# Keys and values first, activations and leaf sums in PSUM, and another order of the last down products

## The chip, the cores and the metric

One Trainium2 chip; the kernel runs on one core. The metric is the device time of one execution in microseconds (us). TensorE is PE, VectorE DVE, ScalarE ACT, GpSimd POOL, SyncE (which here only starts transfers) SP.

## The reference, cut to what matters

```python
def unit_projection(x):                     # query, keys, values
    f = jnp.fft.fft(x); f = f / (jnp.abs(f) + 1e-08); return jnp.fft.ifft(f).real
query = unit_projection(x @ Wq.T + bq)      # x: layernormed, 2 x 4096 x 512
keys, values = unit_projection(x @ Wk.T + bk), unit_projection(x @ Wv.T + bv)
s = jnp.cumsum(bind(keys, values), axis=1)  # bind: product of the spectra
x1 = x0 + unbind(s, query)                  # times the conjugate spectrum
logits = layernorm(x1) @ W_in.T + b_in      # 8 trees of 255 nodes, depth 7
# in each tree, walk from the root by (logit > 0); keep silu(logit) on the path
out = x1 + (silu(logits) * on_path) @ W_out.T
```

## The kernel before, in words

The kernel works through 8192 tokens in NB = 32 blocks of T = 256 (J = 2 halves of 128). Each engine has a program of its own, written out by hand and coupled to the others by semaphores only: `first()` is the prologue, `step(0)`, a loop of steps 1 to 29, and `step(30)`, `step(31)`. In step i a block's feed-forward part runs beside the spectral part of block n = i+1. Nothing reorders an engine's instructions, so the order of the calls is the schedule.

**PE** in a step: `project` for the three groups Q, K, V (144 matmuls into two banks `bank_p`, emptied by ACT's `evac_re` and `evac_im`); `logits(i, t, c)` for tree t, half c (12 matmuls each into `bank_l[t % 4]`), between them `counts(i, t)`, which puts nodes off the path out of play according to the decisions `dec`; `nyquist_rows` and `nyquist_sums` (a few tiny matmuls for one frequency that is handled apart); `down(i, j)`, 42 matmuls for each half j into `bank_l[j]`; then `inverse_transform` into `bank_i[j]`. Operands are split into a high and a low float16 part, and products of three pairs summed: thus the pairs of names `a_hi`/`a_lo`, `xn_pair`, `z_hi`/`z_lo`.

**DVE** in a step: `residual` (x1 = input + inverse transform), statistics and normalisation to `xn2` (L1107), `low` (L1126, the low part of the split), `decide` (L1219, `dec` from the logits), `act_low` (L1226, the low part of the activations), the spectral `q_inverse`, `kv_denominator`, `kv_inverse`, `k_scale` (L1136 to L1154), `running_sum` (L1199, L1202), `next_stats` (layernorm of block n+1), `leaf_dots` (L1239) and `leaf_add` (L1249) for two of the eight trees, whose 128 leaves are not multiplied densely: the row of the reached leaf is fetched by an indirect transfer of POOL into `fetched`, its logit is a dot product with `xn2`, and its output row is added to x1. `result` (L1287) adds the down product, and SP stores it.

**ACT** in a step: the copies out of `bank_p`, squares (L749) and roots (L753), the high halves of splits (L721), `leaf` (L761), `silu(i, t)` (L794) from `bank_l` into `acts`, a ring of HELD = 3 in SBUF, and `act_high` (L804) from `acts`. Sqrt and Silu lie in different function tables: a load of a table (ACT_TABLE_LOAD) stands before the first silu and before the first Sqrt of a step. **POOL** sums squares, forms `bind`, `q_unit`, `unbind`, and starts the fetches.

**Waits that matter.** Normalised halves reach PE through SP's transposing transfers, `xt` (spectral) and `x2t` (feed-forward): `logits(i, 0, 0)` waits for `x2t`, whose transposes wait for `low`; `project(n+1, .)` waits for `xt`. `logits` of tree t reuses `bank_l[t % 4]`, so trees 4 to 7 wait for `silu` of tree t-4 (`act_ready`), `counts(i, t)` for `decide(i, t)`, `down` for `act_low`.

**The prologue** transforms the weights by the DFT on PE (`bias_fold`, `fold_tile`; L473 and L478 spread the largest weight over the partitions), scales and splits W_in and W_out into high and low parts (ACT `win_high`, `wout_high`, L811; DVE `win_low`, `wout_low`, L1327; four pieces each), and does the spectral part of block 0 (`first_bind`, `first_unbind`, `first_z_low` at L1399).

## Time and profile before

| | |
|---|---|
| time before, median of 3 runs | 1904.76 us (1904.72 to 1905.31) |
| the profiled execution's own time | 1902.03 us |
| its span in the profile | 1899.9 us |
| PE busy | 1846.0 us, 97% of the span |
| DVE, ACT, POOL busy | 1548.9, 1117.4, 943.0 us |
| mean granted clock of PE | 0.989 of full speed |

The span runs from the first to the last recorded instruction; the profiled execution's own time has 2.1 us around it. A line is busy time, not importance: PE sets the time wherever it is not idle, and for the rest one has to see what it waits for.

### The profile page before, as it was taken

How to read it: one execution, taken by the hardware profiler on the slowest of the kernel's cores; microseconds unless marked ns; L12 is line 12 of the kernel's file. 1: busy time of each engine (PE TensorE's matmuls, PEld its weight loads, DVE VectorE, ACT ScalarE, POOL GpSimd, SP SyncE). 2: the span in 40 equal slices, each digit the busy share in tenths (PEclk: the TensorE clock that was granted, in tenths of full speed). 3: DMA queues.
4: the chain of work that ended last, by engine and by line, in shares of the span. 5: the costliest groups of instructions: out<-in, count | busy, mean ns of one | idle time of the engine just before them, and what ended most of it. 6: DMA issues, size and time to landing. Idle time of an engine off the chain costs nothing.

```text
span 1899.9 us, 40007 instructions
## 1 busy us (share of the span) xinstructions
PE 1846.0 (97%) x14488; PEld 1389.5 (73%) x14488; DVE 1548.9 (82%) x2938; ACT 1117.4 (59%) x2151; POOL 943.0 (50%) x737
## 2 busy tenths in 40 slices
PE   8499999999999999999999999999999999999978
PEld 6478777778777778877777877777877777787755
DVE  4888888888888888888888888888888888888783
ACT  5666565566565556656556656556655555665643
POOL 1254445564445565444556445556544556545450
PEclk9799999999999999999999999999999999999999
DMA  8032232222133222223222213322223322222312
GB/s 288 12 87 79 68 100 92 74 88 88 55 100 100 70 85 88 73 82 100 79 87 87 85 59 100 98 68 88 88 59 96 100 77 77 88 69 86 89 56 67
DMA packets 181785, 163.18 MB, mean 86 GB/s; under 512 B 140161, under 2 KB 140801, under 8 KB 181761
## 3 DMA queue, kind: packets, MB, share of 16 engines
q1 hardware_dynamic: 163328, 95.48, 17.0%
q0 software_dynamic: 18432, 67.38, 10.7%
q8 instruction: 15, 0.25, 0.1%
q14 instruction: 10, 0.07, 0.0%
HBM read 95.72 MB, written 16.78 MB: 59 GB/s over the span
## 4 chain that ended last, share of the span: by engine, by line
PE 90%; DVE 2%; DMA 1%; ACT 1%; issue 0%; SPq 0%; DVEq 0%; ACTq 0%
PE bank_l L532 31%; PE bank_l L589 30%; PE bank_p L482 23%; PE bank_l L542 3%; PE bank_i L482 2%; DMA arena<-xn_pair 1%; PE bank_i L553 1%; PE bank_i L560 0%; SPq L341 0%; DVE xn_pair L1126 0%; DVE arena L1239 0%; ACT xn_pair L721 0%; ACT arena L794 0%; PE bank_i L559 0%; DVE arena L1249 0%
## 5 line engine op out<-in xcount | busy, mean ns | idle before, releaser
L532 PE MATMUL bank_l<-arena,win_mem 128*128 128x256 f16 x5376 | 625.1, 273 | 16.5 <-DMA arena<-xn_pair 16.5
L589 PE MATMUL bank_l<-wout_mem,arena 128*128 128x512 f16 x2688 | 593.4, 379 | 0.0
L532 PEld LDWEIGHTS bank_l<-arena,win_mem 128*128 128x128 f16 x5376 | 525.0, 98 | 80.5 <-DMA arena<-xn_pair 15.1
L482 PE MATMUL bank_p<-arena,wf_hi 128*128 128x256 f16 x3072 | 505.8, 273 | 2.7 <-ACT arena L740 2.7
L589 PEld LDWEIGHTS bank_l<-wout_mem,arena 128*128 128x128 f16 x2688 | 260.6, 98 | 308.8 <-DVE arena L1226 11.7
L482 PE MATMUL bank_p<-arena,wf_lo 128*128 128x256 f16 x1536 | 419.0, 273 | 0.0
L985 POOL TENSOR_TENSOR arena<-arena 128x512 f32<-128x512 f32 x96 | 121.8, 1269 | 553.1 <-ACT arena L749 553.1
L482 PEld LDWEIGHTS bank_p<-arena,wf_hi 128*128 128x128 f16 x3072 | 299.6, 98 | 37.6 <-ACT arena L740 3.0
L1226 DVE SCALAR_TENSOR_TENSOR arena<-arena,s_act 128x512 f16<-128x512 f32 (+1 forms) x256 | 238.7, 942 | 80.4 <-ACT arena L804 66.3
L794 ACT ACTIVATE arena<-bank_l,bias_in,s_logit 128x256 f32<-128x256 f32 x448 | 229.2, 554 | 121.4 <-PE bank_l L542 121.0
L1219 DVE TENSOR_SCALAR dec<-bank_l,thr,off 128x256 bf16<-128x256 f32 x256 | 136.0, 542 | 92.5 <-PE bank_l L532 91.0
L1066 POOL DMA_INDIRECT arena<-in_leaf_rows,leaf_row x128 | 140.3, 1096 | 109.4 <-issue 70.5
L804 ACT ACTIVATE arena<-arena,s_act 128x512 f16<-128x512 f32 (+1 forms) x256 | 166.6, 664 | 3.2
L482 PEld LDWEIGHTS bank_p<-arena,wf_lo 128*128 128x128 f16 x1536 | 150.5, 98 | 17.5
L1136 DVE RECIPROCAL arena<-arena 128x256 f32<-128x256 f32 x64 | 111.9, 1748 | 61.8 <-POOL arena L990 61.8
L1126 DVE TENSOR_TENSOR xn_pair<-arena,xn_pair 128x512 f16<-128x512 f32 x128 | 143.3, 1142 | 9.5 <-ACT xn_pair L721 9.5
L1239 DVE SCALAR_TENSOR_TENSOR arena<-arena 128x512 f32<-128x512 f32 x128 | 142.7, 1167 | 0.9 <-DMA arena<-in_leaf_rows,leaf_row 0.9
L990 POOL TENSOR_SCALAR arena<-arena,eps_s 128x512 f32<-128x512 f32 x64 | 45.4, 709 | 133.3 <-ACT arena L753 130.3
L1148 DVE RECIPROCAL arena<-arena 128x256 f32<-128x256 f32 x64 | 107.7, 1725 | 1.1
L714 ACT ACTIVATE arena<-arena 128x512 f16<-128x512 f32 x31 | 19.5, 630 | 149.1 <-POOL arena L1030 149.1
L726 ACT ACTIVATE arena<-bank_p,bias_f 128x256 f32<-128x256 f32 x192 | 80.5, 470 | 42.0 <-PE bank_p L482 42.0
L749 ACT ACTIVATE arena<-arena 128x1024 f32<-128x1024 f32 x96 | 101.5, 1057 | 5.3
(175 smaller groups left out, 2500.6 us busy)
## 6 DMA issues: line engine op xcount, KB each, us to landing
arena<-in_x SPq DMA_DIRECT2D x32, 512.0 KB, 3.5
arena<-arena SPq DMA_DIRECT2D x32, 512.0 KB, 2.9
out<-arena SPq DMA_DIRECT2D x64, 256.0 KB, 2.1
wout_mem<-in_w_in_t SPq DMA_DIRECT2D x1, 3584.0 KB, 16.1
arena<-in_w_out_t SPq DMA_DIRECT2D x1, 3584.0 KB, 13.8
arena<-xn_pair SPq DMA_TRANSPOSE x128, 2.8
arena<-in_leaf_rows,leaf_row POOLq DMA_INDIRECT x128, 5.7
win_mem<-in_wq SPq DMA_DIRECT2D x1, 1024.0 KB, 7.5
```

The source lines that it names most:

```text
L482: mm = pe.matmul(bank, a, b, start=(n == 0), stop=(n == len(pairs) - 1))
L532: mm = pe.matmul(bank_l[t % 4][:, c * T:(c + 1) * T], a[:, k, w:w + P], x2t[:, :, b, k, :], start=(c == 0 and k == 0 and m == 0), stop=((t ...
L589: mm = pe.matmul(bank_l[j][:, :], a[:, m, tok], w[:, m, :], start=(m == 0 and a is a_hi and w is wout_hi), stop=(m == DENSE - 1 and a is a ...
L794: ins = act.activation(acts[:, t % HELD, c * T:(c + 1) * T], bank_l[t % 4][:, c * T:(c + 1) * T], ACT.Silu, bias=bias_in[:, c, t:t + 1], s ...
L804: act.activation(a_hi[:, m:m + wide, :], acts[:, t % HELD, 0:wide * T].rearrange("p (c t) -> p c t", c=wide), ACT.Copy, scale=s_act[:, 0:1 ...
L985: pool.tensor_tensor(mag[:, q].rearrange("p c t -> p (c t)"), sq[:, 0:2].rearrange("p c t -> p (c t)"), sq[:, 2:4].rearrange("p c t -> p ( ...
L1066: pool.indirect_dma_start(fetched[:, g, j, :], None, leaf_rows, bass.IndirectOffsetOnAxis(leaf_row[:, g, j:j + 1], 0)).then_inc(leaf_fetch ...
L1126: dve.tensor_tensor(xn_pair[:, j, 1, :], xn[:, j, :], xn_pair[:, j, 0, :], ALU.subtract).then_inc(done, 1)
L1136: dve.reciprocal(mag[:, Q, h], mag[:, Q, h]).then_inc(rinv_ready, 1)
L1219: dve.tensor_scalar(dec[:, t % HELD, :], bank_l[t % 4][:, 0:T], thr[:, t:t + 1], off[:, 0:1], ALU.is_gt, ALU.mult).then_inc(dec_ready, 1)
L1226: dve.scalar_tensor_tensor(out=a_lo[:, m, :], in0=acts[:, t % HELD, 0:wide * T].rearrange("p (c t) -> p c t", c=wide), scalar=s_act[:, 0:1 ...
L1239: ins = dve.scalar_tensor_tensor(out=row, in0=row, scalar=1.0, in1=xn2[:, j, :], op0=ALU.mult, op1=ALU.mult, accum_out=leaf_dot[:, g, j:j ...
```

## The change

- **Group order.** K, V, Q in place of Q, K, V: in the prologue's loads, in `project`, in the spectral work. In the prologue the unbinding is done with the raw query spectrum (`first_unbind`, POOL `first_sums`), and the query's inverse size multiplied in afterwards (`first_unit`).
- **Activations in PSUM.** `acts` is gone: `silu` writes back into `bank_l[t % 4]`, `act_high` and `act_low` read it there; trees 4 to 7 therefore wait for `act_low` of tree t-4 (`a_lo_ready`).
- **xn2 and the leaf sums in PSUM.** `xn2` lies in `bank_i`. `leaf_add` sums into `total` in `bank_l[2 + j]`, begun by an ACT copy of x1 (`begin_total`). `leaf_add(i)` and `result(i)` move into DVE's next step: one `leaf_add` ahead of `residual`, the rest behind `low2`.
- **Down.** Each half is cut in two: trees 0 to 5 of half 0, `counts` 6 and 7, trees 0 to 5 of half 1, then trees 6 and 7 of both. Counts and logits interleave in another order.
- **ACT.** `std(n + 1)` (a Sqrt) moves from ahead of the first silu to between `act_high(4)` and `silu(5)`.
- **Prologue.** All W_out splitting moves out of the prologue into block 0; two W_in pieces of DVE move behind `first_z_low`.
- **SP.** In step i the transposes of `xt` for n+1 now come first and those of `x2t` for block n follow, so that the latter no longer stand behind another copy and load.

The diff, cut to its core (12 leading spaces taken off):

```diff
-HELD = 3
+HELD = 4
...
-Q, K, V, G_IN, G_OUT = range(5)
+K, V, Q, G_IN, G_OUT = range(5)
...
-        sp_size = bank_i[1][:, 16:16 + 3 * J].rearrange("p (j q) -> p j q", q=3)
+        xn2 = [bank_i[j][:, :] for j in range(J)]
+        total = [bank_l[2 + j][:, :] for j in range(J)]
+        sp_rows = bank_p[1][:, 0:3 * J].rearrange("p (j q) -> p j q", q=3)
...
+sp.dma_start(wnat_s[:, K], wk.rearrange("(k p) d -> p k d", p=P)).then_inc(proj_in[K], 16)
 sp.dma_start(dft_s, dft.rearrange("(k p) f -> p k f", p=P)).then_inc(dft_in, 16)
-sp.dma_start(b_nat[:, :, :], b_qkv).then_inc(dft_in, 16)
+sp.dma_start(b_nat[:, :, :], b_kvq).then_inc(dft_in, 16)
+sp.dma_start(xa, x_v[0]).then_inc(x_loaded, 16)
+sp.dma_start(wnat_s[:, V], wv.rearrange("(k p) d -> p k d", p=P)).then_inc(proj_in[V], 16)
 sp.dma_start(wnat_s[:, Q], wq.rearrange("(k p) d -> p k d", p=P)).then_inc(proj_in[Q], 16)
-sp.dma_start(xa, x_v[0]).then_inc(x_loaded, 16)
-sp.dma_start(wnat_s[:, K], wk.rearrange("(k p) d -> p k d", p=P)).then_inc(proj_in[K], 16)
-sp.dma_start(wnat_s[:, V], wv.rearrange("(k p) d -> p k d", p=P)).then_inc(proj_in[V], 16)
...
-    project(0, Q)
+    project(0, K)
...
+    project(0, V)
     for m in range(1, KT):
-        fold_tile(V, m)
-    project(0, K)
-    project(0, V)
+        fold_tile(Q, m)
+    project(0, Q)
...
-    peak_to_all(G_OUT)
     pe.wait_ge(z_hi_ready, 2)
     pe.wait_ge(z_lo_ready, 2)
+    for j in range(J):
+        inverse_transform(j)
+    peaks_in_row(G_OUT)
     pe.wait_ge(sp_carry_ready, 1)
-    for j in range(J):
-        inverse_transform(j)
...
     if attn:
+        project(n, K)
+    if isinstance(i, int) and i == 0:
+        peak_to_all(G_OUT)
+    if attn:
+        project(n, V)
+    if attn:
         project(n, Q)
-        project(n, K)
-        project(n, V)
     logits(i, 0, 0)
+    logits(i, 2, 0)
+    counts(i, 0)
     logits(i, 1, 0)
-    counts(i, 0)
-    logits(i, 2, 0)
     logits(i, 2, 1)
     logits(i, 3, 0)
+    if attn:
+        nyquist_rows(n)
     logits(i, 3, 1)
     counts(i, 1)
+    counts(i, 2)
     logits(i, 4, 0)
+    logits(i, 4, 1)
+    counts(i, 3)
+    logits(i, 5, 0)
+    logits(i, 5, 1)
     leaf_rows_of(i, 0)
-    if attn:
-        nyquist_rows(n)
-    logits(i, 4, 1)
-    logits(i, 5, 0)
-    counts(i, 2)
-    logits(i, 5, 1)
-    counts(i, 3)
+    counts(i, 4)
     logits(i, 6, 0)
+    counts(i, 5)
     logits(i, 6, 1)
-    if attn:
-        nyquist_sums(n)
-    counts(i, 4)
-    counts(i, 5)
     logits(i, 7, 0)
     logits(i, 7, 1)
+    down(i, 0, range(0, 6))
     counts(i, 6)
-    down(i, 0)
-    down(i, 1)
+    counts(i, TREES - 1)
+    if attn:
+        nyquist_sums(n)
+    down(i, 1, range(0, 6))
+    down(i, 0, range(6, TREES))
+    down(i, 1, range(6, TREES))
     if attn:
         transform_back(i)
...
+def high2(n, j):
+    act.wait_ge(ln2_done, J * n + j + 1)
+    act.activation(xn_pair[:, j, 0, :], xn2[j], ACT.Copy).then_inc(xn2_hi_ready, 1)
+def begin_total(i, j):
+    act.wait_ge(a_lo_ready, TREES * i + 7 + j)
+    act.activation(total[j], x1[:, j, :], ACT.Copy).then_inc(total_begun, 1)
...
-    if t >= HELD:
-        act.wait_ge(a_lo_ready, TREES * i + t + 1 - HELD)
-    elif not isinstance(i, int) or i:
-        act.wait_ge(a_lo_ready, TREES * i)
     for c in [c for c in range(2) if (t, c) in COLUMN]:
-        ins = act.activation(acts[:, t % HELD, c * T:(c + 1) * T], bank_l[t % 4][:, c * T:(c + 1) * T],
+        ins = act.activation(bank_l[t % 4][:, c * T:(c + 1) * T], bank_l[t % 4][:, c * T:(c + 1) * T],
...
     act.activation(a_hi[:, m:m + wide, :],
-                   acts[:, t % HELD, 0:wide * T].rearrange("p (c t) -> p c t", c=wide), ACT.Copy,
+                   bank_l[t % 4][:, 0:wide * T].rearrange("p (c t) -> p c t", c=wide), ACT.Copy,
...
-    for c in range(PIECES):
+    for c in range(3):
         wout_rows(c)
-    high(1, xn1, ln1_done, xn1_hi_ready)
     act.wait_ge(z_sum, 1)
     act.activation(z_hi[:, 0:2, :], prod[:, 0], ACT.Copy).then_inc(z_hi_ready, 1)
     act.activation(z_hi[:, 2:4, :], prod[:, 2], ACT.Copy).then_inc(z_hi_ready, 1)
-    wout_high(0)
-    wout_high(1)
+    wout_rows(3)
...
+    if isinstance(i, int) and i == 0:
+        wout_high(0)
+    if attn:
+        square(n, K)
+        evac_im(n, V)
+        square(n, V)
         evac_re(n, Q)
+        root(n, K)
+    if isinstance(i, int) and i == 0:
+        wout_high(1)
+    if attn:
...
+        act.wait_ge(ffn_consts_done, 1)
     if isinstance(i, int) and i == 0:
         wout_high(2)
         wout_high(3)
...
+    silu(i, 0)
     if isinstance(i, int) and i == 0:
-        act.wait_ge(ffn_consts_done, 1)
-    leaf(i, 0)
-    if nxt:
-        std(n + 1, mv1, rs1, ln1_mv, ln1_std)
-    if attn:
-        root(n, V)
-    if isinstance(i, int) and i == 0:
-        act.wait_ge(wout_lo_done, PIECES)
-    silu(i, 0)
+        act.wait_ge(wout_hi_done, 1)
+        act.wait_ge(wout_lo_done, 1)
+    act_high(i, 0)
+    if attn:
+        nyquist_size(n)
+    silu(i, 1)
     leaf(i, 1)
-    act_high(i, 0)
-    silu(i, 1)
-    if attn:
-        nyquist_size(n)
+    act_high(i, 1)
     silu(i, 2)
-    act_high(i, 1)
     act_high(i, 2)
     silu(i, 3)
     leaf_row_copy(i, 0)
+    silu(i, 4)
     act_high(i, 3)
-    silu(i, 4)
     act_high(i, 4)
     if nxt:
+        std(n + 1, mv1, rs1, ln1_mv, ln1_std)
+    silu(i, 5)
+    if nxt:
         shifted(n + 1)
-    silu(i, 5)
     act_high(i, 5)
     silu(i, 6)
     act_high(i, 6)
-    silu(i, 7)
     if nxt:
         act.wait_ge(x2t_ready, 16 * J * (i + 1))
         high(n + 1, xn1, ln1_done, xn1_hi_ready)
+    silu(i, 7)
     act_high(i, 7)
+    begin_total(i, 0)
     if attn:
         z_high(n)
     leaf_silu(i, 0)
+    begin_total(i, 1)
     leaf_silu(i, 1)
 steps(act, first, step)
...
+        sum_squares(n, Q)
+        add_eps(n, Q)
+        bind(n)
         q_unit(n)
-        bind(n)
-    fetch(i, 1)
-    fetch(i, 0)
+    for g in range(LEAVES):
+        fetch(i, g)
...
-                             in0=acts[:, t % HELD, 0:wide * T].rearrange("p (c t) -> p c t", c=wide),
+                             in0=bank_l[t % 4][:, 0:wide * T].rearrange("p (c t) -> p c t", c=wide),
...
-    nyquist_den(0)
-    kv_denominator(0)
-    nyquist_inverse(0)
-    kv_inverse(0, 0)
-    nyquist_unit(0)
     kv_inverse(0, 1)
...
-    low(1, xn1, xn1_hi_ready, xn1_lo_ready)
...
     running_sum(0)
-    peak_row(G_OUT)
     first_unbind()
+    q_inverse(0, 0)
+    q_inverse(0, 1)
+    first_unit()
+    nyquist_den(0)
+    nyquist_inverse(0)
+    nyquist_unit(0)
+    nyquist_bind(0)
+    first_z_low()
+    win_low(2)
...
-    feed_forward_constants()
-    first_z_low()
-    wout_low(0)
-    wout_low(1)
...
+    begun = not isinstance(i, int) or i > 0
+    if begun:
+        leaf_add(i - 1, 0)
+    residual_of(i, 0)
+    if isinstance(i, int) and i == 0:
+        peak_row(G_OUT)
+    residual_of(i, 1)
+    stats2(i)
+    if isinstance(i, int) and i == 0:
+        win_low(3)
+        scale_group(G_OUT)
+    normalise2(i)
+    low2(i)
+    if isinstance(i, int) and i == 0:
+        feed_forward_constants()
+        wout_low(0)
+        wout_low(1)
+    if begun:
+        leaf_add(i - 1, 1)
+        result(i - 1, 0)
+        result(i - 1, 1)
+    if attn:
+        kv_denominator(n)
+    if isinstance(i, int) and i == 0:
+        dve.wait_ge(ffn_consts_done, 1)
+    decide(i, 0)
+    if attn:
+        kv_inverse(n, 0)
+        kv_inverse(n, 1)
+    decide(i, 1)
     if isinstance(i, int) and i == 0:
         wout_low(2)
+    decide(i, 2)
+    if attn:
+        q_inverse(n, 0)
+    if isinstance(i, int) and i == 0:
+        dve.wait_ge(wout_lo_done, 2)
+    act_low(i, 0)
+    if isinstance(i, int) and i == 0:
         wout_low(3)
     if attn:
-        q_inverse(n, 0)
+        k_scale(n)
+        nyquist_den(n)
+    act_low(i, 1)
+    decide(i, 3)
+    if attn:
+        q_inverse(n, 1)
+        nyquist_inverse(n)
+    decide(i, 4)
+    act_low(i, 2)
+    decide(i, 5)
+    if attn:
+        nyquist_unit(n)
     if nxt:
         next_stats(n + 1)
-    decide(i, 0)
-    decide(i, 1)
-    if attn:
-        q_inverse(n, 1)
-        kv_denominator(n)
-        kv_inverse(n, 0)
-        kv_inverse(n, 1)
-        k_scale(n)
-    act_low(i, 0)
-    decide(i, 2)
-    decide(i, 3)
-    if attn:
-        nyquist_den(n)
-        nyquist_inverse(n)
-        nyquist_unit(n)
-    decide(i, 4)
-    decide(i, 5)
+    act_low(i, 3)
+    act_low(i, 4)
+    decide(i, 6)
+    if attn:
+        nyquist_bind(n)
     if nxt:
         scale_and_shift(n + 1)
-    act_low(i, 1)
-    if attn:
-        nyquist_bind(n)
-    act_low(i, 2)
-    act_low(i, 3)
-    decide(i, 6)
     if attn:
         running_sum(n)
-    act_low(i, 4)
+    act_low(i, 5)
     decide(i, 7)
-    act_low(i, 5)
     act_low(i, 6)
     if attn:
         nyquist_unbind(n)
+    leaf_dots(i, 0)
     act_low(i, 7)
+    if attn:
+        nyquist_carry(n)
     if nxt:
         low_of(n + 1, 0, xn1, xn1_hi_ready, xn1_lo_ready)
-    if attn:
-        nyquist_carry(n)
-    if nxt:
         low_of(n + 1, 1, xn1, xn1_hi_ready, xn1_lo_ready)
-    leaf_dots(i, 0)
     leaf_dots(i, 1)
-    leaf_add(i, 0)
     if attn:
         carries(n)
-    leaf_add(i, 1)
-    result(i, 0)
-    result(i, 1)
-steps(dve, first, step)
+def last():
+    for g in range(LEAVES):
+        leaf_add(NB - 1, g)
+    result(NB - 1, 0)
+    result(NB - 1, 1)
```

What stands on the engines now, at three places. **DVE in block 0**, from `low` of the feed-forward layernorm to the first `decide` (L1219, after: L1293); `wout_mem<-arena,sc,wout_mem` is `wout_low`. Before:

```order
L1126 TENSOR_TENSOR xn_pair<-arena,xn_pair 128x512 [waits xn2_hi_ready] x2
L1327 SCALAR_TENSOR_TENSOR wout_mem<-arena,sc,wout_mem 128x1792 [waits scaled,wout_hi_done] x2
L1136 RECIPROCAL arena<-arena 128x256 [waits den_ready]
L1094 BN_STATS st1<-arena 128x6 [waits x_loaded]
L1094 BN_STATS st1<-arena 128x6
L1100 BN_AGGR mv1<-st1 128x2 [waits ln1_stat]
L1100 BN_AGGR mv1<-st1 128x2
L1219 TENSOR_SCALAR dec<-bank_l0,thr,off 128x256 [waits logit_full]
L1219 TENSOR_SCALAR dec<-bank_l1,thr,off 128x256 [waits logit_full]
```

After:

```order
L1404 SCALAR_TENSOR_TENSOR wout_mem<-arena,sc,wout_mem 128x1792 [waits scaled,wout_hi_done] x2
L1216 SCALAR_TENSOR_TENSOR arena<-arena,eps_s 128x512 [waits root_ready,den_ready]
L1293 TENSOR_SCALAR dec<-bank_l0,thr,off 128x256 [waits logit_full,ffn_consts_done]
L1222 RECIPROCAL arena<-arena 128x256 [waits kv_den_ready] x2
L1293 TENSOR_SCALAR dec<-bank_l1,thr,off 128x256 [waits logit_full]
L1404 SCALAR_TENSOR_TENSOR wout_mem<-arena,sc,wout_mem 128x1792 [waits scaled,wout_hi_done]
L1293 TENSOR_SCALAR dec<-bank_l2,thr,off 128x256 [waits logit_full]
L1210 RECIPROCAL arena<-arena 128x256 [waits den_ready]
L1300 SCALAR_TENSOR_TENSOR arena<-bank_l0,s_act,arena 128x256 [waits a_hi_ready,wout_lo_done]
```

Two `wout_low` stand ahead of the first `decide` still, but nothing of them is done in the prologue any more; the feed-forward constants came to this place too.

**ACT in step 0** (the loop's body reads the same there), around the Sqrt on `mv1` that belongs to the next layernorm. Before:

```order
L761 ACTIVATE on_leaf<-bank_l0,one,off_inv 128x256 [waits leaf_row_full,count_full]
L693 ISA
L694 ACTIVATE rs1<-mv1,ln_eps 128x2 [waits ln1_mv]
L753 ACTIVATE arena<-arena 128x512 [waits ss_ready]
L794 ACT_TABLE_LOAD [waits a_lo_ready]
L794 ACTIVATE arena<-bank_l0,bias_in,s_logit 128x256 [waits count_full]
```

After, between `act_high(4)` and `silu(5)`:

```order
L838 ACTIVATE arena<-bank_l3,s_act 128x512 [waits act_ready]
L838 ACTIVATE arena<-bank_l0,s_act 128x512 [waits act_ready]
L712 ISA
L713 ACT_TABLE_LOAD
L713 ACTIVATE rs1<-mv1,ln_eps 128x2 [waits ln1_mv]
L826 REGISTER_ALU
L828 ACT_TABLE_LOAD
L828 ACTIVATE bank_l1<-bank_l1,bias_in,s_logit 128x256 [waits count_full]
```

The Sqrt stood among other Sqrts; now it stands between silus, with a table load on either side of it.

**PE at the end of step 0**: the down matmuls are L589 (after: L597), the counts L542 (after: L554). Before:

```order
L589 MATMUL bank_l0<-wout_mem,arena 128x512 [waits a_lo_ready]
L589 MATMUL bank_l0<-wout_mem,arena 128x512 x5
L542 MATMUL bank_l3<-dec,path 128x256 [waits dec_ready]
L542 MATMUL bank_l3<-dec,path 128x256
L589 MATMUL bank_l0<-wout_mem,arena 128x512 [waits a_lo_ready]
L589 MATMUL bank_l0<-wout_mem,arena 128x512 x5
L589 MATMUL bank_l0<-wout_mem,arena 128x512 [waits a_lo_ready]
L589 MATMUL bank_l0<-wout_mem,arena 128x512 x5
```

After:

```order
L597 MATMUL bank_l0<-wout_mem,arena 128x512 [waits a_lo_ready]
L597 MATMUL bank_l0<-wout_mem,arena 128x512 x5
L554 MATMUL bank_l2<-dec,path 128x256 [waits dec_ready]
L554 MATMUL bank_l2<-dec,path 128x256
L554 MATMUL bank_l3<-dec,path 128x256 [waits dec_ready]
L554 MATMUL bank_l3<-dec,path 128x256
L568 MATMUL bank_p1<-sp_kv,running 128x3 [waits sp_kv_ready]
L569 MATMUL bank_p1<-sp_kv,running 128x3
L597 MATMUL bank_l1<-wout_mem,arena 128x512 [waits a_lo_ready,wout_lo_done,wout_hi_done]
L597 MATMUL bank_l1<-wout_mem,arena 128x512 x29
L597 MATMUL bank_l0<-wout_mem,arena 128x512 [waits a_lo_ready]
L597 MATMUL bank_l0<-wout_mem,arena 128x512 x5
L597 MATMUL bank_l0<-wout_mem,arena 128x512 [waits a_lo_ready]
```

Trees 6 and 7 of half 0 (the rows with waits at the end) now come behind 30 matmuls of half 1.

## Rows read from the trace of the kernel before

**Rows 1.** PE's waits: waited for, us in total, times, longest us.

```profile
PE bank_l L532 <- DMA arena<-xn_pair: 16.5, 5, 14.1
PE bank_l L473 <- DVE mxp L1297: 11.7, 1, 11.7
PE bank_i L482 <- DVE arena L1399: 6.4, 1, 6.4
PE bank_p L434 <- DVE b_pair L1406: 5.1, 1, 5.1
PE bank_i L553 <- ACT arena L740: 4.6, 1, 4.6
PE bank_p L482 <- ACT arena L740: 2.7, 1, 2.7
```

**Rows 2.** Windows; us, busy (x) of PE PEld DVE ACT POOL, clock, DMA share, GB/s.

```profile
60.20:90.00 29.80, 5.84 (x39) 5.06 (x38) 26.93 (x53) 19.32 (x25) 2.97 (x3) 0.57 0.08 18
90.00:109.41 19.41, 16.72 (x147) 14.44 (x145) 16.08 (x35) 12.76 (x22) 2.55 (x3) 0.96 0.34 83
109.41:149.98 40.57, 40.57 (x307) 28.52 (x305) 36.43 (x58) 22.80 (x45) 27.81 (x21) 1.00 0.21 66
302.37:1822.00 1519.63, 1517.52 (x12080) 1143.95 (x12078) 1266.07 (x2395) 906.21 (x1776) 798.35 (x619) 1.00 0.27 83
```

**Rows 3.** The chain that ended last, two steady blocks: start us, us, work.

```profile
358.68 15.65 PE bank_l L589 x72
375.69 15.72 PE bank_p L482 x144
415.00 15.65 PE bank_l L589 x72
```

**Rows 4.** Timeline of DVE in the prologue.

```profile
9.31 1.23 DVE L1293 TENSOR_TENSOR arena<-win_mem 128x1024 f32<-128x1024 f32 x1 [4.34 <-DMA win_mem<-in_wq]
```

**Rows 5.** DVE by line and form: busy us, mean ns | idle before.

```profile
L1226 DVE SCALAR_TENSOR_TENSOR arena<-arena,s_act 128x512 f16<-128x512 f32 x192 | 207.9, 1096 | 74.2 <-ACT arena L804 60.2 <-issue 13.9
L1219 DVE TENSOR_SCALAR dec<-bank_l,thr,off 128x256 bf16<-128x256 f32 x256 | 136.0, 542 | 92.5 <-PE bank_l L532 91.0
L1136 DVE RECIPROCAL arena<-arena 128x256 f32<-128x256 f32 x64 | 111.9, 1748 | 61.8 <-POOL arena L990 61.8
L1327 DVE SCALAR_TENSOR_TENSOR win_mem<-wout_mem,sc,win_mem 128x1792 f16<-128x1792 f32 x4 | 9.9, 2486 | 1.9 <-ACT win_mem L811 1.9
L1327 DVE SCALAR_TENSOR_TENSOR wout_mem<-arena,sc,wout_mem 128x1792 f16<-128x1792 f32 x4 | 8.2, 2083 | 0.9 <-ACT wout_mem L811 0.9
```

**Rows 6.** ACT by line and form: busy us, mean ns | idle before.

```profile
L794 ACT ACT_TABLE_LOAD x32 | 41.1, 1283 | 0.6
L721 ACT ACTIVATE xn_pair<-arena 128x512 f16<-128x512 f32 x128 | 73.3, 621 | 27.9 <-DVE arena L1107 27.9
L811 ACT ACTIVATE wout_mem<-arena,sc 128x1792 f16<-128x1792 f32 x4 | 6.9, 1777 | 0.2 <-DVE sc L1320 0.2
```

**Rows 7.** Timeline of DVE in a steady block: start us, us, work.

```profile
248.00 0.21 DVE L1184 SCALAR_TENSOR_TENSOR sp_z<-bank_i,sp_carry,sp_hat 128x2 f32<-128x2 f32 x1
249.31 1.79 DVE L1226 SCALAR_TENSOR_TENSOR arena<-arena,s_act 128x512 f16<-128x512 f32 x1 [1.10 <-ACT arena L804]
...
278.50 1.22 DVE L1094 BATCH_NORM_STATS2 st<-arena 128x6 f32<-128x512 f32 x2
...
280.13 0.54 DVE L1219 TENSOR_SCALAR dec<-bank_l,thr,off 128x256 bf16<-128x256 f32 x1
...
411.96 0.73 DVE L1226 SCALAR_TENSOR_TENSOR arena<-arena,s_act 128x512 f16<-128x512 f32 x1
```

**Rows 8.** Timeline of POOL at the same time as the first two of rows 7.

```profile
247.61 1.60 POOL L1022 TENSOR_TENSOR arena<-arena 128x512 f32<-128x512 f32 x1
```

**Rows 9.** Timeline of ACT around a table load.

```profile
282.73 0.63 ACT L753 ACTIVATE arena<-arena 128x512 f32<-128x512 f32 x1 [0.22 <-POOL arena L985]
283.38 1.28 ACT L794 ACT_TABLE_LOAD   x1
```

336 lines of the change are left out of this document (187 added, 149 removed).

## The prediction

> **What bounds the kernel now.** I looked first at the table of time and busy shares: PE is busy for 1846.0 of 1899.9 us, so at most 53.9 us can be won while its matmuls stay as they are, and the change takes no matmul away. Next, PE's waits [rows 1]. The reader is to see that nearly all of them happen once: seven or eight single waits of the prologue, 11.7 us for the largest weight of W_out (L473) at their head, and one of 14.1 us, which is the last block, where no projection of a next block hides its normalisation. Of the 16.5 us on `x2t` only 16.5 - 14.1 = 2.4 are spread over four steady blocks. Then the windows [rows 2]: from 302.37 to 1822.00 PE is idle for 1519.63 - 1517.52 = 2.1 us. From 60.20 to 90.00 it is busy for 5.84 of 29.80 us, and its granted clock is 0.57 there, near its lower level of 1.2 GHz; DVE is busy for 26.93 of them. So DVE bounds that stretch, and PE the rest. The chain [rows 3] gives the steady period: 415.00 - 358.68 = 56.32 us.
>
> So the steady blocks have almost nothing to give, and thirty of them multiply whatever goes wrong: 0.1 us a block is 3 us. The prologue can give some.
>
> **Part 1, the prologue.** The order of waits is the DVE's. Before, PE starts the folds once DVE has done the query rows, the first at 9.31 [rows 4], behind a wait for the transfer of wq; after, wk is loaded first and the DFT table second, the bias fold needs the latter, and I let it start at the same point as before plus 0.4 us (it waits longest of the loads now). Before, PE had finished the folds and all of `project(0)` at 60.20 [rows 2]. After, the same matmuls run in another order, with the query group last, and it waits for the last `fold_low` of the query weights, which by DVE's order I place at 57.4, a stall of about 2.3 us: the end is 60.2 + 0.4 + 2.3 = 62.9.
>
> DVE from 57.4, by the durations of its own rows [rows 5] and of those like them: `kv_inverse` 1.75, `k_scale` 1.2, `first_bind` 2.4, the scans 2.7, `first_unbind` 2.5, two `q_inverse` of 1.75 and a short wait 3.7, `first_unit` 1.2, the Nyquist terms 0.9, z 2.7 with ACT's part between: 19.05, of which I take 18.4, since PE, POOL and ACT overlap a little at the joints. The transform begins at 75.8 and takes 1.4 with some reloads; `project(1, K)` starts at about 79.2, where `project(1, Q)` stood at 90.0 [rows 2]: a gain of **10.8 us**. A cross-check from what leaves DVE's stretch: four `win_low` of 2.49 us, of which two come earlier, beside PE's work, and two later; a normalisation and its split, 2.4; the peak of W_out, about 1.5; and two reciprocals of the query come in, 3.5: -9.9 - 2.4 - 1.5 + 3.5 = -10.3. With it go PE's wait of 11.7 us for W_out's peak and the 1.2 and 6.4 after it [rows 1]; one wait of PE for z takes their place.
>
> **Part 2, block 0 pays for it.** What left the prologue is not gone: four `wout_low` of 2.08 us, four `wout_high` of 1.78 us and two `win_low` lie in block 0 [rows 5, 6]. Where do they stand on PE's path?
> - ACT has `wout_high(0)` and one square ahead of `evac_im` of V and `evac_re` of Q: PE waits about 2.35 us for its bank, where it waited 2.7 before [rows 1]. Even.
> - DVE has `wout_low(0)` and `(1)` and the constants ahead of `decide(0)`: 4.2 us, of which 2 lie beside two sets of logits. Stall at `counts(0)` 2.25 us. What is queued behind: `decide(1)` and (2).
> - `decide(2)` stands behind `wout_low(2)`: 0.2 us. `act_low(0)`, which `logits(4)` now waits for since the activations lie in the bank itself, stands behind `wout_high(2)`, `(3)` on ACT and behind the reciprocal of Q on DVE: 1.9 us.
> - `decide(3)` stands behind `wout_low(3)`, `k_scale` and `act_low(1)`: 1.7 us.
>
> That sums to 6.05 us; before, the same block had no wait at all from 109.41 to 149.98 (PE busy 40.57 of 40.57) [rows 2]. Net of prologue and block 0: -10.8 - 0.35 + 6.05 = -5.1, and I take **-4.8** (POOL's tensor work is at its heaviest in that block). Bounds: if all six are hidden -11; if each wait comes out half as long again, and the fold starts 2 us late, 0.
>
> **Part 3, the steady block: what is removed.** Trees' activations, xn2 and the leaf sums come from PSUM. DVE's `act_low` takes 1.096 us in the mean but 0.73 when it is alone [rows 5, 7]. The trace shows who stretches it: at 249.31 an `act_low` with two SBUF inputs took 1.79 us beside POOL's tensor operations, but at 248.00, inside POOL's 1.60 us operation, one with an input in PSUM took 0.21 [rows 7, 8], as its mean elsewhere. So with `acts` in PSUM `act_low` should take 0.73 to 0.8 throughout: 6 of 1.1 become 6 of 0.75, 2 us of DVE a block; `low2` and `leaf_dots` gain likewise, another 1 to 1.5. The rate on a large tile is not shown by a 2-column row; its bounds are 0.73 and 1.1.
>
> The Trainium skill ("SBUF — State Buffer", section "Who interferes with whom") says that a DVE instruction with two SBUF inputs contends with a GpSimd instruction that reads SBUF, and one with at most one SBUF input does not; by that rule the lower bound holds, and the trace's 0.21 us agrees.
>
> All this is off the path, since PE is the bound. What PE gets of it is only the 2.4 us of `x2t` waits: `low2` ends about 0.8 us earlier (`result` and half of the `leaf_add` no longer stand ahead of `residual`; `leaf_add(0)` alone does), and the transposes no longer stand behind the copy and the load on SP's queue. **-2.4**.
>
> **Part 4, the steady block: what is added.** Two more table loads of 1.28 us [rows 6, 9] and two copies of x1 at 0.6 (like the 0.62 of L721) on ACT: 3.8 us a block, on an engine that is busy for 59%. And several tighter waits. From the start of project at t = 0: 144 matmuls 15.72 us [rows 3], so 0.109 each; 12 matmuls of a logits half 1.31, counts 0.22. Then `logits(7, 0)` is due at 15.7 + 12 x 1.31 + 6 x 0.22 + 0.5 = 33.3. It waits for `act_low(3)`; before, it waited for `silu(3)` only, an operation and a half earlier. DVE's chain to it: `logits(5, 1)` ends at 30.2, `decide(5)` 0.2 + 0.5, Nyquist 0.1, `next_stats` 1.63 (280.13 - 278.50) [rows 7], `act_low(3)` 0.73: 33.3. There is no slack. `counts(3)` has 0.1 to 0.2, `logits(4)` and `(6)` 0.5 each. These are sums of ten terms, so their error is some 0.2 us, and a stall of 0.1 repeats 30 times. I take 0.03 a block, **+1**; bounds 0 and 0.4 a block (12 us).
>
> ACT's load before `silu(5)` delays `act_high(5)` and `act_low(5)`, for which tree 5 of `down` on half 0 waits. By the same count it is due 1.4 us after it is ready: that is the cover, and each us beyond it costs 30.
>
> The Trainium skill ("ScalarE: Activation LUTs", section "What ACT_TABLE_LOAD costs") prices a switch at about 1.28 us plus 1.38 us of drain, 2.66 together, and so speaks against two more switches a block. The trace shows the load alone: the root ends at 283.36, the load runs from 283.38 for 1.28 us [rows 9]. By the page, ACT would have 2.8 us more in each block and `act_low(5)` would be late by 1.2 us.
>
> **Part 5, the tail.** The last block's 14.1 us stay; its normalisation writes PSUM and one `leaf_add` precedes its residual: **+0.3**, bounds 0 and 0.6.
>
> **Sum.** -4.8 - 2.4 + 1 + 0.3 = -5.9 against the profiled execution's 1902.03, and the median of the runs shown is 2.7 us above that. 1904.76 - 5.9 = 1898.9; I say **1899.2** (-0.3%). A difference of 0.2%, 3.8 us, is about what a measurement of this kernel can tell from none.
>
> **Rivals.**
> - *A, the orders hold* (forecast): 1895 to 1902. For it: the period is PE's and the slacks add up to zero or more. Chance 0.5.
> - *B, block 0 pays less.* Its waits are mostly hidden since the starts of ACT and DVE move forward with the earlier PE: 4 to 7 us less, 1892 to 1895. Against: the DVE work there is a sum of known durations. Chance 0.1.
> - *C, small loss.* The chain to `logits(7, 0)` or `counts(3)` is 0.1 to 0.2 us late per block (3 to 6 us), or the prologue gains half: 1902 to 1908. For it: slack 0.0. Chance 0.18.
> - *D, the DVE queue becomes the bound* between `decide(5)` and `act_low(3)` (slower side). Place: `next_stats` ahead of `act_low(3)`. It decides from 0.2 us late a block on; at 0.4 it costs 12: 1911. What speaks for it: four banks are now held until `act_low`, where a ring of three and the bank were before. Against: `act_low` from PSUM is alone in 0.73. Chance 0.14.
> - *E, ACT's extra work shows.* If a table switch took the longer of the two times above, or PSUM operands gave no relief from POOL (`leaf_dots(1)` and the split for `xt` then end 1 to 1.5 us late for the transform), 30 blocks lose 1 to 1.5 us each: 1930 to 1945. Against: 283.38 and 248.00. Chance 0.08.
>
> **How the numbers follow.** Faster by over 0.2% (under 1901.0): most of A and all of B, 0.55. Within 0.2%: the rest of A and the first half of C, 0.20. Slower (over 1908.6): the end of C, D and E, 0.25. The range reaches from B's end, 1892, to D's, 1911, and leaves out E and the far part of D.
>
> **What the profile after would show.** Right: the wait of 11.7 us is gone and the first transform begins near 76, after one wait for z; PE waits in block 0 for `dec` and `a_lo`, 6 us in all; `act_low` 128x512 at 0.73 to 0.8 in the mean; PE's period 56.32 still, no repeated wait over 0.1 us; 4 table loads a block of 1.28, each following at once. Wrong: a wait of PE on `act_low` or `decide` 30 times, above all at `logits(7, 0)`; a wait for `z_lo` or `xt` at the end of each block; `act_low` still at 1.1.

## The result, and the profile after

The changed kernel took 1891.05 us in the median of 5 runs (1890.91 to 1896.20), the kernel before 1904.76 (1903.68 to 1905.51): ratio 0.9935, 95% interval 0.9921 to 0.995. In a second series it was 1892.61 against 1903.96, ratio 0.9945 (0.9931 to 0.9959). So the change gives 11 to 14 us, 0.6 to 0.7%, where 5.6 were forecast. The profiled execution took 1893.18 us, its span is 1891.4. The ratios are formed without two slow runs, one of the kernel before (3646.56 us, in the second series) and one of the kernel with the DFT table first (6878.83 us).

The page after, busy time and instructions; beside the table of before: PE 4 us less with the same instructions, DVE 180 us less, ACT 109 us more.

```profile
PE 1842.0 (97%) x14488; PEld 1391.5 (74%) x14488; DVE 1368.7 (72%) x2938; ACT 1226.1 (65%) x2275; POOL 866.8 (46%) x737
```

PE's waits after (us in total, times, longest), which answer to [rows 1]:

```profile
PE bank_l L544 <- DMA arena<-xn_pair: 14.6, 1, 14.6
PE bank_p L568 <- DVE sp_kv L1253: 10.2, 1, 10.2
PE bank_p L442 <- DVE b_pair L1494: 9.1, 1, 9.1
PE bank_l L554 <- DVE dec L1293: 4.1, 2, 2.8
PE bank_p L491 <- issue: 1.9, 1, 1.9
PE bank_l L544 <- DVE arena L1300: 1.7, 1, 1.7
PE bank_p L562 <- ACT arena L778: 1.6, 1, 1.6
PE bank_p L491 <- ACT arena L778: 1.0, 1, 1.0
PE bank_i L491 <- DVE arena L1482: 0.6, 1, 0.6
```

Every wait is a single one, or two in block 0. Of `x2t` (L544) only the last block's is left. The wait of 10.2 us is PE's wait in the prologue for the spectral terms of the one frequency that is handled apart, behind the whole chain of DVE; it takes the place of the one for z.

I cut both traces at the same events: the start of the first projection, of the second, of the third (block 0 lies between the last two) and of the last one. Windows of the kernel before, then after (us; busy and instructions of PE, PEld, DVE, ACT, POOL; granted clock):

```profile
34.10:89.95 55.85, 31.89 (x226) 26.13 (x224) 41.94 (x73) 35.20 (x49) 12.01 (x7) 0.77 0.18 56
89.95:149.89 59.94, 57.25 (x450) 42.91 (x449) 52.47 (x92) 35.56 (x67) 30.36 (x23) 0.99 0.25 71
149.89:1785.22 1635.33, 1633.48 (x12996) 1230.67 (x12994) 1364.30 (x2582) 977.12 (x1914) 860.63 (x667) 1.00 0.27 84
```

```profile
37.69:83.16 45.47, 31.12 (x224) 25.00 (x222) 36.83 (x62) 33.43 (x50) 8.39 (x7) 0.84 0.12 30
83.16:148.35 65.19, 58.38 (x451) 42.87 (x451) 49.17 (x101) 41.90 (x72) 28.03 (x23) 0.98 0.22 66
148.35:1775.83 1627.48, 1627.48 (x12996) 1232.65 (x12993) 1198.72 (x2581) 1081.34 (x2030) 794.41 (x667) 1.00 0.29 84
```

| stretch | before | after | difference | forecast |
|---|---|---|---|---|
| start to first projection | 34.10 | 37.69 | +3.6 | +0.4 |
| first to second projection | 55.85 | 45.47 | -10.4 | -11.2 |
| block 0 | 59.94 | 65.19 | +5.25 | +5.7 |
| 29 steady blocks | 1635.33 | 1627.48 | -7.85 | -1.4 |
| last block and end | 114.6 | 115.5 | +0.9 | +0.3 |

The sum is -8.5, the difference of the spans. The forecast column adds up to -6.2; the -5.9 of the forecast has 0.3 us more for block 0, put on by judgment. In the 29 steady blocks PE never idles after (1627.48 of 1627.48), and each lasts 56.12 us, where it was 56.32 [rows 3]. The chain after, the downs from tree 0 of half 1 on and the projections (start us, us, work; 416.08 - 359.96 = 56.12):

```profile
359.96 11.67 PE bank_l L597 x54
373.00 15.72 PE bank_p L491 x144
416.08 11.67 PE bank_l L597 x54
```

Groups of DVE and ACT by line and form, which answer to [rows 5, 6]: `act_low` takes 0.743 us in the mean (1.096 before). The loads of function tables are 62 + 31 + 30, four in a steady block, in place of 32 + 31, two in a block; each still takes 1.283 us.

```profile
L1300 DVE SCALAR_TENSOR_TENSOR arena<-bank_l,s_act,arena 128x512 f16<-128x512 f32 x192 | 139.9, 743 | 209.6 <-ACT arena L838 208.3 <-issue 1.3
```

```profile
L828 ACT ACT_TABLE_LOAD x62 | 79.5, 1283 | 1.1
L940 ACT ACT_TABLE_LOAD x31 | 39.8, 1283 | 0.6
L713 ACT ACT_TABLE_LOAD x30 | 38.5, 1283 | 0.5
```

### The profile page after: what moved, and what is told of

It is laid out like the page before. It is cut to its first block, busy times and chain, and to the rows that moved or that the text cites. A ratio compares the mean times of both kernels' runs of the same rounds, so it can differ in the third digit from the quotient of the medians.

```text
span 1891.4 us, 39940 instructions
## 1 busy us (share of the span) xinstructions
PE 1842.0 (97%) x14488; PEld 1391.5 (74%) x14488; DVE 1368.7 (72%) x2938; ACT 1226.1 (65%) x2275; POOL 866.8 (46%) x737
## 4 chain that ended last, share of the span: by engine, by line
PE 93%; DVE 3%; issue 1%; ACT 0%; DMA 0%; POOL 0%; SPq 0%; DVEq 0%; ACTq 0%
PE bank_l L597 31%; PE bank_l L544 31%; PE bank_p L491 25%; PE bank_l L554 3%; PE bank_i L491 2%; PE bank_p L562 1%; PE bank_p L569 0%; DVE arena L1210 0%; DVE wout_mem L1404 0%; DVE win_mem L1404 0%; PE bank_p L568 0%; DVE arena L1222 0%; ACT wout_mem L845 0%; DMA arena<-xn_pair 0%; DVE bank_i L1186 0%
## 5 line engine op out<-in xcount | busy, mean ns | idle before, releaser
L544 PE MATMUL bank_l<-arena,win_mem 128*128 128x256 f16 x5376 | 624.7, 273 | 16.4 <-DMA arena<-xn_pair 14.6
L597 PE MATMUL bank_l<-wout_mem,arena 128*128 128x512 f16 x2688 | 590.5, 379 | 0.0
L544 PEld LDWEIGHTS bank_l<-arena,win_mem 128*128 128x128 f16 x5376 | 526.5, 98 | 78.3 <-DMA arena<-xn_pair 15.1
L597 PEld LDWEIGHTS bank_l<-wout_mem,arena 128*128 128x128 f16 x2688 | 263.2, 99 | 302.9
L1024 POOL TENSOR_TENSOR arena<-arena 128x512 f32<-128x512 f32 x96 | 123.1, 1282 | 677.9 <-ACT arena L787 677.9
L828 ACT ACTIVATE bank_l<-bank_l,bias_in,s_logit 128x256 f32<-128x256 f32 x448 | 225.2, 536 | 187.8 <-PE bank_l L554 184.8
L1300 DVE SCALAR_TENSOR_TENSOR arena<-bank_l,s_act,arena 128x512 f16<-128x512 f32 (+1 forms) x256 | 167.8, 666 | 238.2 <-ACT arena L838 236.8
L1293 DVE TENSOR_SCALAR dec<-bank_l,thr,off 128x256 bf16<-128x256 f32 x256 | 133.2, 524 | 46.1 <-PE bank_l L544 46.1
L1114 POOL DMA_INDIRECT arena<-in_leaf_rows,leaf_row x128 | 133.0, 1039 | 72.5 <-ACT leaf_row L810 38.1
L838 ACT ACTIVATE arena<-bank_l,s_act 128x512 f16<-128x512 f32 (+1 forms) x256 | 158.4, 633 | 4.3
L1076 POOL TENSOR_TENSOR arena<-arena 128x512 f16<-128x512 f32 x62 | 93.3, 1523 | 70.5 <-ACT arena L733 70.5
L1343 DVE SCALAR_TENSOR_TENSOR fold<-bank_i,sp_z,odd 128x64 f32<-128x64 f32 (+1 forms) x128 | 35.4, 277 | 102.4 <-ACT odd L758 93.5
L758 ACT ACTIVATE odd<-bank_i 128x256 f32<-128x256 f32 x64 | 24.6, 384 | 128.8 <-PE bank_i L491 128.8
L1047 POOL TENSOR_TENSOR arena<-arena 128x512 f32<-128x512 f32 x31 | 39.3, 1267 | 128.1 <-DVE arena L1228 128.1
```

The costliest lines, as they stand in the source:

```text
L544: mm = pe.matmul(bank_l[t % 4][:, c * T:(c + 1) * T], a[:, k, w:w + P], x2t[:, :, b, k, :], start=(c == 0 and k == 0 and m == 0), stop=((t ...
L597: mm = pe.matmul(bank_l[j][:, :], a[:, m, tok], w[:, m, :], start=(m == 0 and a is a_hi and w is wout_hi), stop=(m == DENSE - 1 and a is a ...
L828: ins = act.activation(bank_l[t % 4][:, c * T:(c + 1) * T], bank_l[t % 4][:, c * T:(c + 1) * T], ACT.Silu, bias=bias_in[:, c, t:t + 1], sc ...
L838: act.activation(a_hi[:, m:m + wide, :], bank_l[t % 4][:, 0:wide * T].rearrange("p (c t) -> p c t", c=wide), ACT.Copy, scale=s_act[:, 0:1] ...
L1024: pool.tensor_tensor(mag[:, q].rearrange("p c t -> p (c t)"), sq[:, 0:2].rearrange("p c t -> p (c t)"), sq[:, 2:4].rearrange("p c t -> p ( ...
L1114: pool.indirect_dma_start(fetched[:, g, j, :], None, leaf_rows, bass.IndirectOffsetOnAxis(leaf_row[:, g, j:j + 1], 0)).then_inc(leaf_fetch ...
```

## Experiments

Two questions: where the 0.20 us a steady block come from, and why the start pays another amount than worked out. The theory after the first reading: in the kernel before, PE waited in each block 0.107 us for the low part of tree 7's activations, ahead of the 37th down matmul of half 0 (this comes from the starts of single matmuls, which the views merge; the table of waits leaves out so short a one). DVE's row is the `act_low` that starts at 418.26, takes 1.80 us beside POOL, and ends at 420.06, just ahead of that matmul's start at 420.11:

```profile
418.26 1.80 DVE L1226 SCALAR_TENSOR_TENSOR arena<-arena,s_act 128x512 f16<-128x512 f32 x1 [1.09 <-ACT arena L804]
```

Either the split of the down products hides the wait (theory S) or activations in PSUM shorten what it waits for (theory P).

**The changed kernel again.**

> The changed kernel once more, unaltered, to be the standard for the other runs of this series. In its profile the steady period was 56.12 us without a repeated wait, against 56.32 before. Both theories below expect 56.12 again. The profiled execution was 2.2 us above the timed median; if the difference lies in the prologue (the granted clock of PE rises only at about 23 us there), this profile shows another start of the second projection than 83.16 us, and the same period.

Period 56.12 again, PE without a wait in the steady blocks. The profiled span was 1889.4, 2 us shorter, and all of it lies ahead of the first projection: it starts at 35.39 in place of 37.69. The rows are the first folds of weights on PE (start us, us), of the kernel after and of the same kernel again:

```profile
18.02 1.21 PE L469 MATMUL bank_l<-arena 128*128 128x257 f32 x2
19.88 1.23 PE L474 MATMUL bank_l<-arena 128*128 128x257 f32 x2
```

```profile
17.98 1.19 PE L469 MATMUL bank_l<-arena 128*128 128x257 f32 x2
19.52 0.70 PE L474 MATMUL bank_l<-arena 128*128 128x257 f32 x2
```

The same two matmuls take 1.23 us or 0.70. PE begins at about half its pace and comes to the full one at another moment in each execution, though it is busy without a gap meanwhile (12.00 of the 12.00 us from 12 to 24 in the first profile) and the granted clock reads 1.00 in these windows. Such a pair first takes 0.70 us at 19.52 in this profile, at 24.16 in the first one, and at 28.61 in the profile of the run without the root's table loads; the first projections start at 35.39, 37.69 and 39.58. So about half of the time by which the full pace comes later is lost. The eight profiles with this prologue start the first projection at 35.2 to 35.5 us five times, at 37.7 twice and at 39.6 once. What sets the moment is open.

**The down products whole.** The changed kernel with the down products in the order of the kernel before.

```diff
-down(i, 0, range(0, 6))
 counts(i, 6)
+down(i, 0, range(0, 3))
 counts(i, TREES - 1)
 if attn:
     nyquist_sums(n)
-down(i, 1, range(0, 6))
-down(i, 0, range(6, TREES))
-down(i, 1, range(6, TREES))
+down(i, 0, range(3, TREES))
+down(i, 1, range(0, TREES))
```

> The changed kernel with the down products in the order of before (half 0 whole, with the counts of tree 7 inside it, then half 1). In the kernel before, PE waited in every block for the low part of the activations of tree 7, 0.107 us by the starts of single matmuls, too short for the table of waits. Theory S (the split of the down products hides that wait): without the split it is back, 0.05 to 0.1 us a block or more, period 56.2 or above, 2 to 3 us slower than the changed kernel. Theory P (activations in PSUM make the low part fast enough, 0.75 us against 1.8): no wait, period 56.12, the same time as the changed kernel.

1932.69 us, ratio to before 1.0154 (1.0138 to 1.017): 40 us slower than the changed kernel beside it, far beyond both theories. The wait is another one than either had:

```profile
PE bank_l L554 <- DVE dec L1292: 37.2, 32, 1.3
```

It is the decision of tree 7. DVE makes it behind `act_low(5)` (in the kernel before it stood ahead of it), and that one waits for ACT (timeline of DVE, then of ACT, one block):

```profile
473.16 0.75 DVE L1299 SCALAR_TENSOR_TENSOR arena<-bank_l,s_act,arena 128x512 f16<-128x512 f32 x1 [1.28 <-ACT arena L837]
473.82 0.53 DVE L1292 TENSOR_SCALAR dec<-bank_l,thr,off 128x256 bf16<-128x256 f32 x1
```

```profile
467.22 1.28 ACT L712 ACT_TABLE_LOAD   x1
468.83 1.28 ACT L827 ACT_TABLE_LOAD   x1
```

The period is 57.45. `counts(7)` is due 2.8 us after the logits with the whole down product (`counts(6)` 0.22 and 12 matmuls), 6.7 with the split one (30 matmuls). So what the split hides in the changed kernel is above all the late decision, not tree 7's activations. That the decision is late because of ACT's `act_high(5)` with the two table loads ahead of it, and DVE's new order, is read from this trace; no run has the whole product without the loads.

**The split alone in the kernel before.**

```diff
-down(i, 0)
-down(i, 1)
+down(i, 0, range(0, 6))
+down(i, 1, range(0, 6))
+down(i, 0, range(6, TREES))
+down(i, 1, range(6, TREES))
```

> The kernel before with the split of the down products alone (trees 0 to 5 of half 0, of half 1, then 6 and 7 of both). Theory S: the wait for tree 7 goes, period 56.32 - 0.107 = 56.21, 3 us faster than before. If half 1 or the release of its bank brings a new wait, the same or slower. The rest of the gain of the change, 0.09 us a block, then has another source: the four tiny matmuls of one frequency, which took 0.45 us before and 0.37 after, because they stand elsewhere.

Period 56.21, as expected: the 0.107 us are gone, with the activations still in SBUF. The 72 down matmuls that took 15.65 us [rows 3] take 15.54 (chain):

```profile
361.41 15.54 PE bank_l L590 x72
```

The time is 1901.88 against 1903.96, ratio 0.9991 (0.9981 to 1.0): 2 us where 3 were expected, and by the interval not safely apart from none. PE now waits more often for `x2t` (17.2 us in 8 times, before 16.5 in 5), which takes back part of it.

**Activations in SBUF.** The changed kernel with a ring of four in SBUF; waits and orders unchanged.

```diff
+acts = sb("acts", [P, HELD, 2 * T])
-    ins = act.activation(bank_l[t % 4][:, c * T:(c + 1) * T], ...
+    ins = act.activation(acts[:, t % HELD, c * T:(c + 1) * T], ...
-    in0=bank_l[t % 4][:, 0:wide * T]...
+    in0=acts[:, t % HELD, 0:wide * T]...
```

> The changed kernel with the activations in a ring of four in SBUF again; all waits and orders are those of the changed kernel, so only where an operand lies differs. Theory P: the low part of the activations (128x512) goes from 0.743 back to about 1.1 us in the mean, beside POOL's tensor operations 1.3 to 1.8; the logits of trees 4 to 7 wait for it (they have 0.1 to 0.3 us of slack), so a wait of 0.3 to 1 us appears in each block: 10 to 30 us slower. Theory O (the orders alone make the gain, the operand's place is off the path): the low part gets slower, but the time stays within 2 us of the changed kernel.

1915.72 us, ratio to before 1.0061 (1.0045 to 1.0077), 23 us slower than the changed kernel beside it; period 56.89, 0.77 longer. `act_low` (L1301 there) and PE's wait for it:

```profile
L1301 DVE SCALAR_TENSOR_TENSOR arena<-acts,s_act,arena 128x512 f16<-128x512 f32 x192 | 223.6, 1177 | 164.0 <-ACT arena L839 160.3
```

```profile
PE bank_l L545 <- DVE arena L1301: 12.4, 32, 1.8
```

For `act_low` only the place of one operand differs: 1.177 against 0.743 us, where about 1.1 was expected. Its shortest took 0.72 us, as in PSUM, and its longest 1.85, so SBUF is not slower for it as such. ACT's part moved too (silu writes and `act_high` reads SBUF), but by little: `act_high` takes 0.718 us for 0.686, silu 0.560 for 0.536. The loss lies within the 10 to 30 us that theory P expected, and theory O (the orders alone make the gain) is out: in this order the activations have to be in PSUM. As an explanation of the 0.107 us P is not needed, by the run before.

**Two table loads fewer, two more.** In the first, ACT copies in the steps in place of taking the square root of the next block's variance (its result is a little wrong); in the second two tiny activations (Silu, Sqrt) follow it.

```diff
+def std_copy(n, mv, rs, have, done):
+    act.wait_ge(have, J * (n + 1))
+    act.activation(rs[:, :], mv[:, :, 1], ACT.Identity, bias=ln_eps[:, 0:1],
+                   scale=1.0 / X_SCALE).then_inc(done, 1)
...
-std(n + 1, mv1, rs1, ln1_mv, ln1_std)
+std_copy(n + 1, mv1, rs1, ln1_mv, ln1_std)
```

```diff
 std(n + 1, mv1, rs1, ln1_mv, ln1_std)
+act.activation(warm[:, 0:1], ln_eps[:, :], ACT.Silu)
+act.activation(warm[:, 1:2], ln_eps[:, :], ACT.Sqrt)
```

> The changed kernel with the square root of the next block's standard deviation left out in the steps (ACT copies a scaled variance, so the first layernorm of blocks 2 on is scaled a little wrongly): two of the four table loads of a block go. Theory L0 (the loads are hidden): ACT is busy for 2.6 us less a block, PE's period stays 56.12, the time is the same. Theory L1 (the two loads cost something on the path): faster by up to 0.2 us a block, 6 us.

> The changed kernel with two more table loads and two tiny activations ahead of the fifth tree's silu, 3.0 us more of ACT there (2 x 1.28 and 2 x 0.2). The prediction gave the low part of tree 5's activations a cover of 1.4 us; in the trace after it is 1.55 (468.41 to 469.96). If a load costs its 1.28 us and no more, PE waits 3.0 - 1.55 = 1.4 us a block there or a little less: +40 us over 29 blocks. By the Trainium skill (ScalarE: Activation LUTs, What ACT_TABLE_LOAD costs) each switch costs 2.66 us in all; then the extra work is 5.7 us and the wait over 4 us a block, +120 us. If the cover is larger than I read it, the time is the same.

Without the loads: 1894.61, ratio 0.9949 (0.9934 to 0.9963), period 56.12, nothing gained; they are hidden. With two more: 1937.09, ratio 1.0182 (1.0167 to 1.0197), period 57.64:

```profile
PE bank_l L598 <- DVE arena L1303: 40.3, 30, 1.3
```

The period is 1.52 us longer for 3.0 us more of ACT's work (four loads and their activations in place of two): the cover of `act_low(5)` was 1.5 us, and a load costs its 1.28 us alone.

**Slack ahead of tree 7's logits.**

```diff
 next_stats(n + 1)
+dve.tensor_copy(fold[:, 0:4 * QI], x1[:, 0, 0:4 * QI])
 act_low(i, 3)
```

> The changed kernel with one copy of 128x252 elements more on DVE just ahead of the low part of tree 3's activations, some 0.3 us. The prediction's fourth part gave that chain no slack against the logits of tree 7; the trace after shows about 0.1 us. Theory D (there is no more slack): a wait of 0.15 to 0.3 us at the logits of tree 7 in each block, +4 to +9 us. Rival: the handoff has slack that the trace doesn't show, the time is the same.

The copy was larger than the expectation says: 128x508 elements, 0.67 us, of which DVE's next instruction started 0.58 later (461.96 to 462.54). The period rose by 0.51, to 56.63, with 30 waits of PE for `act_low`. So the slack was 0.07 us, and theory D holds: 29 times 0.51 is 15 us, more than the 4 to 9 expected, as the copy was larger. The time: 1908.17, ratio 1.0026 (1.0015 to 1.0037).

```profile
461.96 0.67 DVE L1621 COPY fold<-arena 128x508 f32<-128x508 f32 x1
462.54 1.40 DVE L1300 SCALAR_TENSOR_TENSOR arena<-bank_l,s_act,arena 128x512 f16<-128x512 f32 x2
```

**The DFT table first.** The changed kernel, but with the loads in the order table, biases, key weights, and the bias pairs formed first by DVE.

> The changed kernel with the DFT table and the biases loaded ahead of the key weights again, and the bias pairs formed first on DVE. In the trace after, PE starts the bias fold at 9.14 us (before at 5.12) and the first fold of weights at 13.16 (before 10.59), and its granted clock rises some 7 us later. Theory F: the late bias fold is what makes the first projection start at 37.7 rather than 34.1; with the table first it starts at 34 to 35 and the second projection at 80 to 81 rather than 83.16: 2 to 3 us faster. Rival: DVE's chain to the last fold of the query weights sets the time, and that does not move: the same.

The bias fold starts at 4.92, the first projection at 32.80, the second at 78.26: 2.4 to 4.9 us earlier than in the two profiles of the changed kernel, span 1886.6. So theory F holds for this execution, by more than the 2 to 3 us expected against the later of them. Among timed runs it hardly shows: 1892.14 in the median (five runs from 1888.44 to 1894.26), ratio 0.9943 (0.993 to 0.9956). That the others lose to PE's half pace what this one won at the start would fit the spread of 5.8 us, but only one execution was profiled.

**The order of block 0.** Lines that moved, for ACT (down to `wout_high(3)`) and DVE in block 0 only:

```diff
 std(i, mv2, rs2, ln2_mv, ln2_std)
+wout_high(0)
...
 high2(i, 1)
-wout_high(0)
+wout_high(1)
...
 root(n, K)
-wout_high(1)
 root(n, V)
+wout_high(2)
...
-wout_high(2)
-wout_high(3)
 silu(i, 0)
...
 act_high(i, 1)
+wout_high(3)
...
 stats2(i)
-win_low(3)
...
 low2(i)
 feed_forward_constants()
 wout_low(0)
+win_low(3)
 wout_low(1)
+decide(i, 0)
 kv_denominator(n)
-decide(i, 0)
...
 act_low(i, 0)
-wout_low(3)
...
 decide(i, 3)
+wout_low(3)
-q_inverse(n, 1)
...
 act_low(i, 4)
+q_inverse(n, 1)
```

> The changed kernel with another order in block 0 only. In the trace after, DVE idles for 5.3 us there (98.5 to 103.8) because the second piece of W_out's high part stands on ACT behind a root that waits for POOL, and PE then waits 2.8 us for the first decision. Here ACT makes the first piece before the value copies and the second behind the split of xn2, DVE decides tree 0 ahead of the keys' denominator, makes the last W_in piece in the idle time, and the last W_out piece after tree 3's decision; one reciprocal of the query moves 5 us later. Theory A (ACT's late piece is the cause of the waits of block 0, 5.8 us in all): from the second to the third projection 61 to 62 us instead of 65.2, 3 to 4 us faster than the changed kernel. Rival (DVE's own work in that block, 12 us more than in a steady one, is the cause): 64 to 65 us, the wait only moves to the logits of tree 4.

> The order of block 0 as in the run before it and the DFT table loaded first. If the two are independent, the gains add: a profiled execution with the second projection at 78 us and the third at 139.5 to 143, span about 1883 to 1886, where the changed kernel's two profiles had 1889.4 and 1891.4. If the earlier start only lets block 0 wait longer, the same as the better of the two alone.

With the new order alone block 0 took 65.8 us, above what either theory expected. With the DFT table first too it took 62.8; the third projection starts at 141.0 and the span is 1885.3, both within what was expected of that run. Windows of the two around PE's waits before the logits of tree 4, each with the stretch after it:

```profile
108.00:111.50 3.50, 0.83 (x7) 0.26 (x4) 3.36 (x5) 3.37 (x8) 1.37 (x1) 0.88 0.00 0
111.50:117.00 5.50, 5.48 (x26) 3.90 (x27) 4.64 (x8) 2.28 (x4) 4.25 (x3) 0.50 0.01 3
```

```profile
105.00:109.00 4.00, 1.36 (x11) 0.73 (x9) 3.86 (x5) 3.87 (x8) 1.90 (x1) 1.00 0.00 0
109.00:115.00 6.00, 5.95 (x58) 5.36 (x59) 5.88 (x10) 3.49 (x7) 4.72 (x3) 1.00 0.01 3
```

With the new order alone PE's granted clock falls to 0.50, its lower level of 1.2 GHz, behind a stretch in which it was busy for 0.83 of 3.5 us; 24 matmuls of the logits take 5.30 us there, 2.79 in the other kernel. With the table first too, the same waits stand there and the clock stays at 1.00. Against the first profile of the changed kernel (65.2 us), whose clock did not fall in this block either, theory A's gain is seen in size: 2.4 of the 3 to 4 us expected, from waits that are 2.9 us shorter. The second profile of the changed kernel has a stretch at 0.50 of its own in block 0, in the query's projection, behind 3.53 us with PE busy for 1.36:

```profile
97.53:100.94 3.41, 3.41 (x18) 2.43 (x17) 0.00 (x0) 3.41 (x5) 1.96 (x2) 0.50 0.48 154
```

So block 0's length alone does not tell one order from another here; one has to take its waits and its clock apart. PE's waits of block 0 fell from 6.35 us (2.17, 1.12, 1.74, 1.32 in the second profile of the changed kernel) to 3.87 (0.72, 0.46, 0.89, 1.80) with the new order alone. Timed: 1891.25 (1890.79 to 1891.70), ratio 0.9937 (0.9923 to 0.995), and 1889.52 (1887.13 to 1889.92), ratio 0.9926 (0.9912 to 0.9939). The last is the fastest kernel of the study by its median; its interval overlaps the changed kernel's.

**Two edits in the kernel before.** The split, and `nyquist_rows` one call later:

```diff
 leaf_rows_of(i, 0)
-if attn:
-    nyquist_rows(n)
 logits(i, 4, 1)
+if attn:
+    nyquist_rows(n)
```

> The kernel before with the split of the down products and, besides, the four small float32 matmuls of the one frequency apart (nyquist_rows) moved from behind the one-column leaf matmuls to behind twelve wide matmuls of the logits. The split alone gave a period of 56.21 us. Theory W (the first float32 weight load of that group, 0.19 us, hides under a wide matmul but not under a one-column one): 56.21 - 0.09 = 56.12, the changed kernel's period, without any operand in PSUM; about 5.5 us faster than before in all. Rival (the 0.09 us belongs to PSUM or to the other orders): the period stays 56.21.

Period 56.12: theory W holds, the other 0.09 us are this. The group of four small matmuls in the chain, in the kernel before and in this one (0.11 us less; the wide matmuls beside it take 0.02 more):

```profile
401.09 0.45 PE bank_i L553 x4
```

```profile
404.01 0.34 PE bank_i L553 x4
```

The time is 1899.81 against 1903.44, ratio 0.9982 (0.9973 to 0.9991): 3.6 us, not 5.5. The steady stretch is 5.0 us longer than 29 periods of 56.12, where the kernel before has 2.05 above 29 of 56.32, since the waits for `x2t` grow:

```profile
151.44:1783.98 1632.54, 1629.45 (x12996) 1230.60 (x12994) 1367.06 (x2582) 977.63 (x1914) 868.24 (x667) 1.00 0.28 84
```

## Why the forecast was right in direction and short in size

The forecast was 1899.2 (1892 to 1911) with case A; it came to 1891.05 in the first series, 1 us below the range, and to 1892.6 in the second, just inside. Both lie where rival B was put (1892 to 1895, chance 0.1), but B's mechanism is not what happened: block 0 paid 5.25 us, nearly all that was worked out. Right were prologue, block 0, and the tight waits of the steady block; wrong were the period, which gave 6.4 us more than forecast, and the start, which took 3.2 more. The two errors partly cancel, so the profiled difference, -8.5 against -6.2 by the stretches, looks better than its parts.

- **The steady period (parts 3 and 4), the step that failed.** The prediction took 56.32 us as PE's own time and said "All this is off the path, since PE is the bound". 0.20 of it was not work: 0.107 us of waiting for `act_low(7)`, below what the table of waits lists, and 0.09 us of a float32 weight load that nothing hid. Over 29 blocks that is 5.8 us. The two edits in the kernel before reach 56.12 with the activations, xn2 and leaf sums still in SBUF: it is the order of PE's calls that shortens the period, and PSUM is what lets this order run without waits.
- **The `x2t` waits.** -2.4 forecast, -2.05 measured (7.85 - 5.8). The last kernel shows that they grow to 5.0 us when PE gets faster; in the changed kernel they are gone. Whether `low2`'s earlier end or SP's new order does that was not tried apart.
- **No slack ahead of `logits(7, 0)` (rival D).** Worked out as 0.0 and charged with +1 us; the slack is 0.07 us, and no wait came of it, so the charge was 0. The chain of ten terms was right within 0.1 us; on which side of zero it fell was luck, since the prediction gave it an error of 0.2.
- **PSUM operands.** `act_low` was put at 0.73 to 0.8 us: it is 0.743 in PSUM, and 1.177 in SBUF with all orders the same. DVE's relief was put too low, 3 to 3.5 us a block in place of 5.7 (1364.30 - 1198.72 over 29 blocks), without a consequence on the path. The Trainium skill's rule (SBUF — State Buffer, Who interferes with whom), that a DVE instruction with at most one SBUF input does not contend with GpSimd, agrees with these two numbers. With the activations in SBUF this order loses 23 us, so rival E rightly made a loss depend on the relief from POOL; it put it at 1 to 1.5 us a block, at the end of the block, and it is 0.77, at the logits.
- **Table loads.** Hidden, with 1.5 us of cover where 1.4 was said. A load costs 1.28 us. The 2.66 us a switch of the Trainium skill (ScalarE: Activation LUTs, What ACT_TABLE_LOAD costs) are not what this trace shows: with two more loads the period grew by 1.52 us, where by that rule PE would wait over 4 a block. (The 1.2 us by which the prediction lets `act_low(5)` be late on that rule should read 1.4, its 2.8 us less the cover of 1.4.)
- **Block 0.** +5.25 against +5.7, but one reason was wrong: I put the wait for `decide(0)` down to DVE's two `wout_low`. DVE idled for 5.25 us there, waiting for ACT's `wout_high(1)`. Between `wout_high(0)` and it, from 96.4 to 102.0, ACT had two squares, five copies and a root to do, and idled for only 0.98 of it, for POOL; so it is ACT's queue that makes it late, and POOL only in small part. The waits themselves came near to what was worked out: 0.97, 2.78, 1.74 and 1.32 us, where 2.35, 2.25, 1.9 and 1.7 were put.

```profile
103.82 2.08 DVE L1404 SCALAR_TENSOR_TENSOR wout_mem<-arena,sc,wout_mem 128x1792 f16<-128x1792 f32 x1 [5.25 <-ACT wout_mem L845]
```

- **The start (part 1).** From the first projection on it was -10.4 against -11.2: DVE's chain from the second `kv_inverse` to z took 19.4 us (60.36 to 79.81), near the 19.05 of the sum and not the 18.4 that were taken for it. But the bias fold, which the prediction let start "at the same point as before plus 0.4 us", waits for 9.14 us in place of 5.1, as DVE takes the key rows first, and the folds follow at half pace for longer: +1.1 to +5.5 by the execution. The profiled executions differ by 8.9 us and the medians by 11 to 14, because the one before was 2.7 us faster than its median and the one after 2.1 slower. It fits that the execution profiled before had an early start (34.10; its edited versions 36.28 and 35.64) and the one after a late one; the executions that make the medians were not profiled.
- **The end.** +0.9 against +0.3, a difference that is within the spread: from the start of the last projection the end took 114.1 to 116.8 us in the profiles of the changed kernel and its edits, 114.5 to 115.6 in the three of the kernel before and its edits. The last matmul starts 4.7 us before the end, before 3.7; but one profile with the changed end (that with the slack) has 3.7 too. What decides it is open.

## What to carry to other kernels

A period equal to the busy time of its engine isn't yet that engine's least: compare the starts of single matmuls in a steady block with their usual pitch (or, in the chain, the time of equal groups), for waits of 0.1 us and small matmuls between wide ones, which the summary of waits doesn't list. Where the order leaves no slack, putting one operand of a DVE instruction in PSUM is worth what POOL takes from it otherwise, here 0.43 us each. Work moved from a prologue in which PE is idle into the first block cost half of its gain again here (5.25 of 10.4 us); look there for who is waited for, not for who has much to do.

## What the runs showed of the hardware

- PE's pace at the start is not the same from one execution to the next: the first pairs of fold matmuls went from 1.23 us to 0.70 at 19.5 us in one profile, at 24.2 in another of the same kernel, and at 28.6 in a third with the same prologue, with a spread of 4.4 us in the start of the first projection (35.2 to 39.6).
- A stretch of 3.5 us in which PE was busy for 0.83 was followed by one of 5.5 us with its clock at 0.50; a similar one, 1.36 busy of 4.0, was not, and another, 1.36 busy of 3.53, was. The 24 matmuls of the first took 2.5 us longer for it (5.30 against 2.79), about as much as the two waits ahead of them (0.89 and 1.80).
- DVE's `act_low` of 128x512 took 0.743 us in the mean with one input in PSUM and 1.177 with both in SBUF; POOL was busy for 923.2 us in the latter run and for 857.7 and 866.8 in the two profiles of the former, so POOL seems to pay too (its times are rough).
- The first float32 weight load (0.19 us) of a group of small matmuls was hidden behind a 128x256 matmul (which starts 0.109 us after the one before) and not behind a one-column one (0.025): 0.09 us a block.
